# Two tiles of the router's normalisation moved one step ahead, and products of the identity in two gaps, in a one-layer language model tower

## The reference

```python
h = tok_embedding(x)                       # position, nesting and segment tables, then W
h = h + attention(layernorm(h))            # 8 heads, causal within a block of 128
z = layernorm(h)
logits = z @ router_w.T + router_b         # 8 experts
topk_val, topk_idx = top_k(logits, 2); weights = softmax(topk_val)
h1, h2 = split(z @ fc1_w[e].T + fc1_b[e]); a = silu(h1) * h2
h = h + sum over the two experts of weight * (a @ fc2_w[e].T + fc2_b[e])
```

## Time and profile before

| | |
|---|---|
| median of 3 runs | 1395.51 us (1392.03 to 1395.72) |
| the profiled execution | 1403.95 us, span 1402.2 us |
| granted TensorE clock, mean | 0.965 |
| busy: PE, PEld | 1185.3 us (85%), 1020.0 us (73%) |
| busy: DVE, ACT, POOL | 1017.6 us (73%), 943.8 us (67%), 879.9 us (63%) |
| chain that ended last | PE 71%, DVE 13%, issue 6%, DMA 2% |

### The profile page before, as it was taken

The page is one execution under the profiler, slowest core; times in us unless marked ns, Lnnn a source line. Parts: engine busy times, 40 slices in busy tenths (PEclk is TensorE's granted clock), DMA queues, the critical chain, the costliest instruction groups (busy, mean ns, idle before and its releaser), DMA issues.

```text
span 1402.2 us, 49716 instructions
## 1 busy us (share of the span) xinstructions
PE 1185.3 (85%) x15049; PEld 1020.0 (73%) x15050; DVE 1017.6 (73%) x3895; ACT 943.8 (67%) x3491; POOL 879.9 (63%) x1178
## 2 busy tenths in 40 slices
PE   6898999999999999999999764787777867778775
PEld 4577777877787777777777654777777767777774
DVE  6579988888888888888888756555555545555553
ACT  2788889888888888888889643444444444444442
POOL 6557877777777777777777543555555535555554
PEclk9899999999999999999999876999999989999998
DMA  4240010101010110101010113544545343333331
GB/s 159 77 181 20 32 47 29 44 30 42 30 41 32 41 34 32 42 32 42 29 46 29 51 47 100 150 147 146 146 143 151 115 124 110 108 113 102 112 107 47
DMA packets 68054, 109.04 MB, mean 78 GB/s; under 512 B 12756, under 2 KB 32948, under 8 KB 67860
## 3 DMA queue, kind: packets, MB, share of 16 engines
q1 hardware_dynamic: 50068, 62.67, 15.9%
q0 software_dynamic: 17920, 45.55, 9.0%
HBM read 45.66 MB, written 54.11 MB: 71 GB/s over the span
## 4 chain that ended last, share of the span: by engine, by line
PE 71%; DVE 13%; issue 6%; DMA 2%; another core or an unknown queue 2%; POOL 1%; ACT 1%; DVEq 1%; POOLq 0%; ACTq 0%; SPq 0%
PE ps L1443 11%; PE ps L1252 10%; PE ps L1254 8%; PE ps L1253 8%; PE ps L1388 8%; PE ps L1401 6%; PE ps L1350 6%; PE ps L1365 3%; DVE v L985 2%; PE ps L1372 2%; DVE xT_lo L1145 2%; PE ps L1355 2%; PE ps L1439 1%; PE ps L1421 1%
## 5 line engine op out<-in xcount | busy, mean ns | idle before, releaser
L776 ACT ACTIVATE probs<-ps,neg_max 128x128 f32<-128x128 f32 (+1 forms) x1024 | 339.2, 357 | 39.5 <-DVE neg_max L979 34.6
L1252 PE MATMUL ps<-xT_hi,w_now 128*128 128x256 f32 x572 | 179.7, 314 | 93.7 <-DVE xT_lo L1145 93.2
L716 ACT CAST xT_hi<-ps 128x256 fp32r<-128x256 f32 x143 | 54.3, 380 | 256.7 <-PE ps L1421 233.2
L776 ACT ACTIVATION_READ_ACCUMULATOR probs<-ps,neg_max 128x1 f32 x1024 | 227.0, 222 | 0.0
L1252 PEld LDWEIGHTS ps<-xT_hi,w_now 128*128 128x128 f32 x572 | 110.5, 193 | 108.6 <-DVE xT_lo L1145 106.3
L677 POOL DMA_INDIRECT xs<-v x108 | 104.0, 963 | 102.1 <-DVE v L1151 71.6
L677 POOL DMA_INDIRECT out_h<-v x108 | 103.8, 961 | 98.5 <-DVE v L1151 70.8
L581 POOL TENSOR_TENSOR probs<-probs,inv_sums 128x384 f32<-128x384 f32 x120 | 99.2, 827 | 103.5 <-DVE inv_sums L919 103.1
L1254 PE MATMUL ps<-xT_hi,w_now 128*128 128x256 f32 x572 | 163.3, 285 | 0.8 <-issue 0.8
L1253 PE MATMUL ps<-xT_lo,w_now 128*128 128x256 f32 x572 | 163.1, 285 | 0.0
L1151 DVE SCALAR_TENSOR_TENSOR v<-ps,v 128x128 f32<-128x128 f32 x216 | 65.7, 347 | 130.8 <-PE ps L1443 125.2
(11 more groups left out here) (248 smaller groups left out, 3275.4 us busy)
## 6 DMA issues: line engine op xcount, KB each, us to landing
v<-xs SPq DMA_DIRECT2D x108, 260.0 KB, 2.6
kT<-xs SPq DMA_DIRECT2D x35, 260.0 KB
xs<-pad_rows SPq DMA_DIRECT2D x16, 520.0 KB, 3.0
normed<-h SPq DMA_DIRECT2D x32, 256.0 KB
w_parts<-in_w SPq DMA_DIRECT2D x1, 2048.0 KB, 9.1
xs<-normed,row POOLq DMA_INDIRECT x128
xs<-v POOLq DMA_INDIRECT x108
out_h<-v POOLq DMA_INDIRECT x108
```

The lines of the kernel that those rows point to most:

```text
L776: ins = nc.scalar.activation(probs_p[par][:, half, slots[n]], ps[:, SCORES + half, slots[n]], ACT.Exp, bias=neg_max[par][:, half, n:n + 1] ...
L1252: T.matmul(dst, w_hi_, x_hi_, start=True, stop=False)
```

## The change

Two tiles of `apply_norm` go from the second step of a group (`route_apply`) to the end of the first (`route_apply_2`, of which only VectorE has a part). In the last octet `route_apply` still does all four. The signal `normed2_ready` is given after the last tile, in the second step, as before. Beside that, TensorE makes 14 products of the 128x128 identity with itself ahead of the first block and 30 ahead of the 73rd, into a bank that holds nothing then. They come after the wait for the table and before the wait for the rows.

```diff
+WARM = (14, 30)
@@ octet_steps
         if n == 0:
             steps += [("stats", half + 2), ("rstd", half + 2)]
             late("route_rows", half - 3)
+            late("route_apply_2", half - 2)
         elif n == 1:
             late("route_apply", half - 2)
@@ VectorE
                 elif kind == "route_scale":
                     raw_logits(G, par)
-                    apply_norm(o, i, par)
+                    apply_norm(o, i, par, range(GB)).then_inc(normed2_ready, 1)
                     add_bias(G)
+                elif kind == "route_apply_2":
+                    apply_norm(o, i, par, range(2))
                 elif kind == "route_apply":
-                    apply_norm(o, i, par)
+                    apply_norm(o, i, par, range(0 if final else 2, GB)).then_inc(normed2_ready, 1)
@@
-            def apply_norm(o, i, par):
+            def apply_norm(o, i, par, tiles):
                 dve.wait_ge(scattered[par], SW_LEAD + 16 * GB * (o + (i - par) // 2))
-                for j in range(GB):
+                for j in tiles:
                     ins = V.tensor_scalar(normed2[par][:, j, 0:D], h2[par][:, j, 0:D], moments2[:, j, 0:1], rstd2[:, j:j + 1],
                                           ALU.subtract, ALU.mult)
-                ins.then_inc(normed2_ready, 1)
+                return ins
@@ TensorE
+            def keep_warm(count):
+                for _ in range(count):
+                    T.matmul(ps[:, H1[0], 0:128], ident[:], ident[:], start=True, stop=True)
+
             for k in range(TOPK):
                 pe.wait_ge(table_ready, LEAD + k + 1)
+                keep_warm(WARM[k])
                 for n in range(2):
                     rows_in(k * PH + n, k * turns, n)
```

## The result

The changed kernel takes 1411.37 us (median of 4 runs, 1408.77 to 1414.1) beside 1394.8 us for the kernel before (1392.03 to 1395.72). The ratio is 1.0138, interval 1.0112 to 1.0163, so 16 to 23 us slower, 19.2 in the middle. The profiled execution took 1413.01 us, span 1411.1.

What follows compares the result with a forecast made beforehand. Attention steps were taken as bound by a ring across engines, the second lengthened by late TensorE signals. Span 1402.2 + 15.4 − 3.1 = 1414.5 us; the 12.3 us change on the median gave 1407.8, range 1385 to 1420.

Steps and rivals of the forecast that it cites:

- The tiles at the end of the first step: Attention stage, first step: two moved tiles cost 0.75 us in one group and 0.55 in the next, 0.65 on average.
- The wait for the scatter: First step: VectorE waits 0.3 us for a scatter of the group before last, in every other group.
- The room ahead of line 1000: First step: VectorE has 0.1 us to spare before the maxima, subtracted from the price in one group of two.
- The guess that the second step wins 0.1 back: Second step: its later start recovers 0.1 us in its own waits, leaving 0.55 a group.
- The count of 28 groups: The move is paid for in octets 1 to 14, 0.55 us × 28 = 15.4 us.
- The second step gains nothing: Second step: the 0.55 us freed on VectorE is worth nothing, since the maxima wait for TensorE's late signal.
- The rival that the release follows VectorE: Second step: maxima start because line 1000 ends, so it gains 0.55 us; 1395.5 us in all, chance 0.20.
- The rival that the signals vanish: Second step: the shift takes TensorE's signal out of the issue's window, gaining 0.88 us; 1386.0 us, chance 0.20.
- the ring: Attention stage: scores, maxima, eight exponentials and next scores wait on each other, needing 5.43 us from maxima to maxima.
- The lock: First step: GpSimd's power operation holds a moved tile, taken as 0; as a rival 29 us on top, 1437 us, chance 0.13.
- The products: Two feed-forward gaps: identity products keep TensorE's clock up for the first two blocks, worth 1.6 and 1.5 us, 3.1 together.
- the products do nothing: Feed-forward gaps: the clock falls again or the products hold back a signal, 3.1 us more, 1410.9 us; chance 0.05.

Runs made afterwards that it cites:

- the idle tiles: Kernel before plus two unread tiles at the end of the first step, without the scatter wait, the second step keeping its four; ratio 1.0061.
- the tiles left out: Kernel before with two of the second step's four normalised tiles left out in 28 groups, their rows staying zero; ratio 1.0011.
- the last run: Kernel before with the two tiles moved and the second step's indirect DMA issued after the residual's addition, no products; 1396.69 us against 1402.45, ratio 0.9963.
- The late issue: Kernel before with the second step's indirect DMA issued after the residual's addition; two runs on the faster kind of chip, ratios 1.0001 and 0.9991.

## Why the prediction was right, and where it was not

The forecast was 1407.8 us, the time is 1411.37, inside the range. The slowdown itself was forecast at 12.3 us and is 16 to 23. By its own steps:

**The tiles at the end of the first step.** Priced at 0.75 and 0.55 us, measured 0.72 and 0.52 (6.25 − 5.53, 6.17 − 5.65). The wait for the scatter was put at 0.3 in every other group; the waits show 4.1 us in 12, that is 0.34. The room ahead of line 1000 was a little larger than the 0.1 assumed: the idle tiles, without a wait, cost 0.31 in the second half's group, so 0.24. The guess that the second step wins 0.1 back was 0.10 and 0.03. The count of 28 groups was two too many: octet 1 took no longer than before.

**The second step gains nothing.** Right, and for the reason given: the gap ahead of the maxima grew by the same half microsecond, and the release stayed 1.5 us after the start of GpSimd's issue. The rival that the release follows VectorE falls with the tiles left out (ratio 1.0011). The rival that the signals vanish falls for this change, since the scores moved with the issue; but its price, a step that drops to the ring at 5.43, is what the last run shows once the issue is moved away (5.42).

**The lock.** Right that the moved tiles are not held: the power operation runs from 424.82 to 425.87 in the group shown above, and the first of the tiles beside it takes 0.34 us. The Trainium skill ("SBUF — State Buffer", the section on its two separate sides) says that of a VectorE operation in a two-port mode and a GpSimd operation, the one that starts first has the shared ports for its whole length and the other fully blocks; for this pair the trace doesn't agree, and the measurement decides. Nor is line 1000 held by the power operation: before the change, in the groups of the first half, it starts 0.04 us behind it and takes 0.56 or 0.57. But I looked at the wrong pair. What the moved tiles bring close together is line 1000 and line 610, GpSimd's scaling of the values, which follows its power operation. In 3 of the 28 first steps of octets 1 to 14 in the kernel after (4 with the move alone, 5 in the last run) the step takes 7.27 us, and all of these groups are in the second half of an octet. One of them, POOL and DVE:

```profile
229.08 0.60 DVE L1095 TENSOR_SCALAR normed<-h,moments,rstd 128x128 f32<-128x128 f32 x2 [0.57 <-DMA xs<-normed,row]
...
229.72 1.03 POOL L612 TENSOR_TENSOR v<-v,rstd 128x512 f32<-128x512 f32 x1
...
229.85 1.31 DVE L1002 TENSOR_TENSOR probs<-probs,inv_sums 128x384 f32<-128x384 f32 x1
```

and the ordinary case:

```profile
425.73 0.56 DVE L1002 TENSOR_TENSOR probs<-probs,inv_sums 128x384 f32<-128x384 f32 x1
...
425.86 1.33 POOL L612 TENSOR_TENSOR v<-v,rstd 128x512 f32<-128x512 f32 x1
```

Where GpSimd's line 610 starts first, line 1000 is held and takes 1.2 to 1.5 us; where line 1000 starts first by 0.03 to 0.2 us, GpSimd is the one held (1.25 to 1.43 for 1.03) and the ring hardly notices. (With the move alone, one group in which line 1000 was 0.02 ahead lost too.) Before the change line 1000 was ahead by 1.46 us in these groups (416.36 in the earlier trace rows), POOL:

```profile
417.82 1.03 POOL L610 TENSOR_TENSOR v<-v,rstd 128x512 f32<-128x512 f32 x1
```

The tiles and the scatter's wait used that up to a margin of 0.2 us or less, and the wait varies between 0.2 and 0.6, so some groups lose. In the groups of the first half, which don't wait, the margin fell from 0.99 to 0.47 and none is held. With the idle tiles, which wait for no scatter, it is 0.53 and 0.48, and none is held either, so it takes the wait to lose the race. The Trainium skill (same page and section) also names VectorE operations with two inputs in SBUF, against a GpSimd operation that reads SBUF; here the trace agrees: line 1000 has two. Even the 1.46 us with which I priced this rival was a held operation: its row starts 0.01 after line 1000's, and without that neighbour the operation takes 1.05. So one of the two reasons for taking the cost as nothing, that line 1000 is not lengthened beside the power operation, was misread: there GpSimd was the one held. Price: 1.02 us in each of 3 steps, 3.1 us that the sum left out.

**The products.** Priced at 3.1 us, worth nothing that can be measured (1.0007, and 1411.37 against 1410.04 us with and without them in separate comparisons). The 14 products took 6.17 us, as worked out (6.0). Two steps failed. "TensorE's work before it is needed is then close behind" was assumed to be enough, but in the first gap the clock fell again behind 14 products and 1.36 us of idle time. The idle time alone does not decide it, since behind 18 products and 1.5 us the clock held. SyncE's load came about 1 us later besides: 14.47 us from table to third block became 15.31. In the second gap I counted 30 products at full clock, 6.4 us; they took 7.84 (clock 0.72 from 1135 to 1140) and ended directly ahead of the transposes. From GpSimd's last issue to the third block it was 9.41 us instead of 10.26, a gain of 0.85; in the run of the products alone it was 11.97, a loss of 1.7 on the same measure, though without products this stretch takes 10.3 to 11.8 us on chips of the late kind, so neither is a price. The rival "the products do nothing" came true for the products. That its time, 1410.9, lies so near the measured one is partly luck, because its 15.4 for the steps lacks the held steps and has two groups too many, where 17.4 was measured.

**The sum.** Steps as measured, in the 26 groups that paid: (0.62 − 0.07) × 26 = 14.3 us, where the forecast had 15.4. Plus 3.1 for the held steps, minus 0 for the products: 17.4 us. The loop's octets in the two traces differ by 16.8, and the ratio says 16 to 23. The 12.3 of the forecast was short by the held steps and by the 3.1 that it counted on from the products, less 1.1 for the two groups too many. The products had the weaker rows: nothing in the trace of before showed the clock after a gap of one or two microseconds, and I took the upper end.

## What to carry to other kernels

Moving work off an engine pays only where that engine ends last in the step it leaves; here the idle time ahead of the next operation, and what released it, told that it did not, and the same half microsecond was lost where it went. Before moving work ahead of an operation that shares ports with another engine's, read the margin between their starts: a margin of 1.5 us cut to 0.2 or less turns a fixed order into a race that costs 1 us each time it is lost. Where two engines are released together and late, look at what GpSimd issues just then: moving one indirect DMA behind the next signal made the same move of tiles go from 1.4% slower to 0.4% faster, each beside the kernel before on its own chip.

## What the runs showed of the hardware

**Chips differ.** The same kernel before took 1390 to 1402 us on some chips and 1243 to 1244 on others, with the same granted clock (mean 0.965 and 0.967 in the two traces) and the same first and third steps within 0.02 us. The second step is 6.29 and 6.22 us on one and 5.68 and 5.60 on the other, the fourth of the first half 5.86 and 5.69, and a feed-forward block 3.6 and 2.65. On the first kind a signal of TensorE that falls beside GpSimd's issue in the second step is seen 1.5 us after the start of the issue (1.53 and 1.49, whether the issue takes 1.05 us or 1.37); on the other it is seen at once (in the feed-forward stage 0.03 us after the end of the transposes). What the two kinds differ in stays open. A time from one kind says little on the other: the move costs 1.4% on one and 0.8% on the other. The late issue without the move was never run on the late kind. With the move it took nearly the same octet on either kind (47.46 us on the late one; the move alone 47.19 on the other); if that holds without the move too, its octet of 46.2 us, measured on the other kind, against 47.73 would make it the better version there. This is argued, not shown.

**Products and a load.** With products of the identity running, SyncE's load started 5.3 to 5.5 us after the table in all three kernels that have them, instead of 3.9 to 4.5 in those without, though nothing in the program ties them. The cause is open, and whether it is the products that delay the load is only as sure as these three traces against eleven.

**The clock after a short idle time.** After 14 products and 1.36 us of idle time the clock had risen and fell again with the first block, and so it did after 14 products and 1.87 us in the run of the products alone; after 18 products and 1.5 us it held for both blocks. After 24 products and 3.05 us it had fallen. These are four rows, so no more than that.
